# Decoder layer on one core: the first two phases rebuilt (weight splits, score blocks, token load, row copies)

## What is computed

```python
x = x + attn(layernorm(x))            # 16 heads of 8, causal softmax, then a layernorm of its own and Wo
x = x + xattn(ctx, layernorm(x))      # one head of 128 over the 64 context tokens, biases bv, bq, bo
x = x + ffn(layernorm(x))             # 8 experts 128 -> 512 -> 128 with relu, b1, b2;
                                      # gates: alpha-entmax (alpha 1.5) of xt @ Wr + br, by 25 bisections
```

## Time and profile before

| what | us |
|---|---|
| median of 3 runs (785.18 to 788.53) | 788.36 |
| profiled execution | 785.36 |
| its span | 783.6 |
| phases 0 and 1, to the first expert product | 163.4 |
| one round of the loop (246.8 to 326.0 is the most of one) | 79.2 |
| PE busy | 693.9 (89%) |

### The profile page before, as it was taken

One profiled execution on the slowest core, in us unless ns is written; L12 is line 12 of the kernel. 1 busy time (PEld: TensorE's weight loads), 2 busy tenths in 40 slices (PEclk: granted clock), 3 DMA queues, 4 the chain that ended last, 5 costly groups with the idle time before them and its releaser, 6 DMA issues.

```text
span 783.6 us, 14820 instructions
## 1 busy us (share of the span) xinstructions
PE 693.9 (89%) x4769; PEld 493.9 (63%) x4769; DVE 454.5 (58%) x953; ACT 419.3 (54%) x800; POOL 349.7 (45%) x571
## 2 busy tenths in 40 slices
PE   4797374679998999999999999999999999988996
PEld 3553243456776677667766776677767775666774
DVE  3246133643698368845875578647954795455542
ACT  3121362148556764576556655675568546755443
POOL 5000244035535654464536353735374517453363
PEclk9977595569999999999999999999999999999998
DMA  6200421003500270017100710062006300500040
GB/s 200 55 1 10 128 58 28 2 16 74 133 2 17 47 173 1 15 25 172 24 3 14 168 50 2 15 143 74 2 15 137 81 2 3 122 17 0 19 104 13
DMA packets 36169, 42.44 MB, mean 54 GB/s; under 512 B 3860, under 2 KB 19745, under 8 KB 36133
## 3 DMA queue, kind: packets, MB, share of 16 engines
q1 hardware_dynamic: 36132, 41.99, 22.2%
HBM read 9.46 MB, written 2.10 MB: 15 GB/s over the span
## 4 chain that ended last, share of the span: by engine, by line
PE 44%; issue 26%; POOL 12%; DVE 7%; ACT 6%; SPq 2%; DMA 1%; POOLq 1%; ACTq 0%; DVEq 0%
PE h_ps L849 6%; POOL y_sb L802 4%; PE h_ps L851 4%; PE h_ps L850 4%; POOL acc L805 3%; PE sbuf_s L931 3%; PE y_ps L849 3%; PE y_ps L851 3%; PE y_ps L850 3%; POOL rstd_a L734 3%; PE sbuf_s L917 3%; DVE negmax L1335 2%; ACT ln L1128 2%; ACT prob L1167 2%; PE sbuf_m L931 2%
## 5 line engine op out<-in xcount | busy, mean ns | idle before, releaser
L1419 DVE SCALAR_TENSOR_TENSOR h_lo<-h_ps,h_hi 128x512 fp32r<-128x512 f32 x256 | 173.9, 685 | 152.3 <-ACT h_hi L1186 150.4
L1186 ACT ACTIVATE h_hi<-h_ps 128x512 fp32r<-128x512 f32 x256 | 153.5, 600 | 159.8 <-PE h_ps L851 157.5
L725 POOL TENSOR_SCALAR_AFFINE_SELECT prob<-prob 128x512 f32<-128x512 f32 x128 | 81.0, 642 | 147.0 <-ACT prob L1167 141.6
L1335 DVE TENSOR_REDUCE negmax<-sbuf_s 128x4 f32<-128x1024 f32 (+1 forms) x96 | 114.3, 1218 | 18.1 <-PE sbuf_s L900 18.1
L1167 ACT ACTIVATE prob<-sbuf_s 128x768 f32<-128x768 f32 x128 | 99.4, 814 | 47.2 <-PE sbuf_s L917 47.1
L849 PE MATMUL h_ps<-fT_lo,w_hi 128*128 128x512 f32 x256 | 118.6, 463 | 5.0 <-DVE fT_lo L1311 2.7
L849 PE MATMUL y_ps<-h_lo,w_hi 128*128 128x512 f32 x256 | 103.1, 403 | 1.2 <-ACT y_sb L1193 1.2
L851 PE MATMUL h_ps<-fT_hi,w_hi 128*128 128x512 f32 x256 | 101.6, 397 | 0.0
L850 PE MATMUL h_ps<-fT_hi,w_lo 128*128 128x512 f32 x256 | 101.5, 397 | 0.0
L851 PE MATMUL y_ps<-h_hi,w_hi 128*128 128x512 f32 x256 | 101.1, 395 | 0.0
L850 PE MATMUL y_ps<-h_hi,w_lo 128*128 128x512 f32 x256 | 101.0, 395 | 0.0
(11 more groups left out here) (327 smaller groups left out, 1120.8 us busy)
## 6 DMA issues: line engine op xcount, KB each, us to landing
gate_b<-gT SPq DMA_DIRECT2D x64, 256.0 KB, 4.9
stacks<-qk SPq DMA_DIRECT2D x96, 128.0 KB, 2.6
x_t<-in_x_dram SPq DMA_DIRECT2D x8, 256.0 KB, 2.8
gate_b<-in_L_ffn_W_dram SPq DMA_DIRECT2D x1, 2048.0 KB
stacks<-qk SPq DMA_DIRECT2D x128, 4.0 KB
x_r<-in_x_dram SPq DMA_DIRECT2D x8, 256.0 KB, 4.0
out_dram<-sums SPq DMA_DIRECT2D x8, 256.0 KB, 4.1
prob<-in_ctx_dram SPq DMA_DIRECT2D x1, 512.0 KB, 4.1
```

The costliest lines, as they stand in the source:

```text
L725: pool.affine_select(out=v, in_=v, compare_op=ALU.is_ge, fill=0.0, base=0, pattern=[[0, 2], [0, 2], [1, P]], channel_multiplier=-1).then_i ...
L1186: act.activation(h_hi[:, c % HB, :], h_ps[:, c % 2, :], ACT.Relu).then_inc(hhi_made, 1)
L1335: dve.tensor_reduce(negmax[:, tile, heads].rearrange("p (g j) -> p j g", j=NJ)[:, j:j + 2, :], halves[buf].rearrange("p j (g s) -> p j g s ...
L1419: dve.scalar_tensor_tensor(out=h_lo[:, c % HB, :], in0=h_ps[:, c % 2, :], scalar=0.0, in1=h_hi[:, c % HB, :], op0=ALU.max, op1=ALU.subtrac ...
```

## The change

Phases 2 to 6 keep their tables. Phases 0 and 1 get new ones, and these things are different in them:

1. W1 is split first, straight from `stage`: four steps w1r, ACT rounds two experts to w1_hi, POOL subtracts to w1_lo. The centring of a w1 step then is two one-pass products on w1_hi and w1_lo, and b1 is a third over two rows (high part and rest). w1 0 and 1 stay in phase 0, w1 2 to 7 are in phase 1. W2's load waits for the splits alone (new step w2L). The last w2 split waits for w1 7 and vo 1.
2. A step "pairs" makes the two-row biases of b1 and xbo. Its source is a copy of b1 to all 128 rows; ACT rounds it, DVE forms the rest on odd rows. It stands behind T1 on ACT.
3. The next tokens' load (XL) is issued before the stack copies; SZ 1 and NZ 1 are in phase 0.
4. MAX and SC work in half blocks in phases 0 and 1: each step has two heads a group and its own buffer.
5. Half of phase 0's stack copies is issued by ACT (new step KS).
6. In every phase the rows of MT go in two copies of 16 rows in place of eight of 4; negmax is laid out for that.
7. ka 0 and 1, kp 1 and vo 1 move from phase 0 to phase 1, and vp 0, xwo and V move ahead in phase 0.

```diff
@@ tables (some rows)
-    Step("Q", 0, "s", pe=2, act=2, dve=2),
-    Step("K", 0, "t", pe=3, act=3, dve=3, sp=3),
-    Step("V", 0, "m", pe=3.1, dve=3.1),
+    Step("pairs", 0, "-", act=0.2, dve=6.2),
+    Step("XL", 1, "-", sp=1),
+    Step("Q", 0, "s", pe=1, act=2, dve=2.1),
+    Step("xwo", 0, "y", pe=3.1, act=1, dve=3),
+    Step("V", 0, "u", pe=3, dve=2),
+    Step("K", 0, "y", pe=6, act=5.1, dve=6.1, sp=4),
+    Step("KS", 0, "-", act=6.1),
...
@@ SP
+            sp.dma_start(whole[:, 0:2 * F], b1.rearrange("(a n) f -> a (n f)", n=2).unsqueeze(1)
+                         .to_broadcast([NE // 2, 32, 2 * F])).then_inc(b_loaded, 16)
...
-                for g in range(NG):
-                    for r, src in enumerate((nm_hi, nm_lo)):
-                        sp.dma_start(words(qs[3 + 4 * r:P:ROWS, g, t]), words(src[g * NJ:(g + 1) * NJ, t]))\
-                          .then_inc(nm_stacked[b], 16)
+                for r, src in enumerate((nm_hi, nm_lo)):
+                    sp.dma_start(words(qs[3 + 4 * r:P:ROWS, :, t]), words(src[:, t])).then_inc(nm_stacked[b], 16)
...
-                    for e in range(NE):
-                        drained(sp, ph, "w1", e)
+                if name == "w2L":
+                    sp.wait_ge(w1_lo_made, NE // 2)
...
@@ POOL
+                if name == "w1r":
+                    c = slice(2 * n, 2 * n + 2)
+                    pool.wait_ge(w1_hi_made, n + 1)
+                    pool.tensor_tensor(w1_lo[:, c, :], stage[:, c, :], w1_hi[:, c, :], ALU.subtract).then_inc(w1_lo_made, 1)
...
@@ PE
+            def heads_of(ph, n):
+                return range(NJ) if ph.f is not None else range(2 * (n % 2), 2 * (n % 2) + 2)
...
-                    last = centred(dst, stage[:, n, :], rows[at:at + 1, n % 2 * F:(n % 2 + 1) * F], at)
+                    r = slice(n // 2 * 32, n // 2 * 32 + 2)
+                    pe.matmul(dst, centre_r, w1_hi[:, n, :], start=True, stop=False)
+                    pe.matmul(dst, centre_r, w1_lo[:, n, :], start=False, stop=False)
+                    last = pe.matmul(dst, share_r[r, :], b1_pairs[r, n % 2 * F:(n % 2 + 1) * F], start=False, stop=True)
...
@@ ACT
+                if name == "pairs":
+                    act.wait_ge(b_loaded, 32)
+                    act.activation(b1_pairs, whole[:, 0:2 * F], ACT.Copy).then_inc(pairs_hi, 1)
+                    act.activation(xbo_pair, whole[:, 2 * F:2 * F + E], ACT.Copy).then_inc(pairs_hi, 1)
...
+                if name == "KS":
+                    drained(act, ph, "Q")
+                    drained(act, ph, "K")
+                    act.wait_ge(const_made, 7)
+                    for r, src in enumerate((qk[:, 0:4:2, :], qk[:, 1:3, :], qk[:, 0:4:3, :])):
+                        for g in range(1, NG, 2):
+                            act.dma_start(words(stacks[r:P:4, :, g, :]), words(src[g * 32:(g + 1) * 32, :, :]))\
+                               .then_inc(stacked, 16)
```

More of the change, by code:

```diff
@@ L291 @@
+    Step("MAX", 10, "s", pe=30.1, dve=31),
+    Step("NA", 2, "-", act=31),
+    Step("SC", 0, "s", pe=31.2, act=31.1, pool=31),
+    Step("MAX", 11, "t", pe=31.1, dve=31.1),
+    Step("MT", 1, "v", pe=33.1, dve=32, sp=34),
+    Step("T3", 0, "m", pe=33, act=33, dve=33),
+    Step("SC", 1, "t", pe=35, act=34, pool=34),
+    Step("SC", 2, "s", pe=35.1, act=34.1, pool=34.1),
+    Step("SC", 3, "t", pe=35.2, act=35, pool=35),
 ]
@@ L333, in in_order, with earlier @@
         return sorted([s for s in self.all if s[place] is not None], key=lambda s: s[place])
+    def earlier(self, engine):
+        return Phase(0, z=0).in_order(engine) if self.parts == self.KINDS[1] else []
     def fill(self, step):
+        if step[0:2] not in self.order[step.buf]:
+            return Phase(0, z=0).fill(step)
         return self.before[step.buf] + self.order[step.buf].index(step[0:2])
     def find(self, name, n=0):
-        return next(s for s in self.all if s[0:2] == (name, n))
+        return next(s for s in self.all + (FIRST_Z if name in TABLES else []) if s[0:2] == (name, n))
     def steps(self, engine, slot):
@@ L891, in max_scores @@
                 for at, g in enumerate(gs):
-                    for j in range(NJ):
+                    for j in js:
                         r = slice(ROWS * j, ROWS * (j + 1))
@@ L911, in scores @@
                     pair = ph.z if n < EARLY else ph.a
-                    pe.wait_ge(nm_stacked[b], pair * 128 + 128)
+                    pe.wait_ge(nm_stacked[b], pair * 32 + 32)
                 for first in (True, False):
-                    for j in range(NJ):
+                    for j in js:
                         r = slice(ROWS * j, ROWS * (j + 1))
@@ L918, in scores @@
                                          qs[r, g, b * S + q0:b * S + q0 + w], start=True, stop=True)
-                        if not first and j == 1:
+                        if not first and j == 1 and len(js) == NJ:
                             last.then_inc(full["s"], 1)
@@ L937, in step @@
                 name, n, buf = s[0:3]
-                if name in ("MAX", "SC") and n % 2:
+                quad = name in ("MAX", "SC") and ph.f is not None
+                if quad and n % 2:
                     return
@@ L1298, in step @@
                     level_xwq()
+                if name == "pairs":
+                    dve.wait_ge(ident_made, 2)
+                    mark(dve.tensor_reduce(odd[:, :], ident[:, 1:P:32], AX.X, ALU.add, negate=True))
+                    settle()
+                    dve.wait_ge(pairs_hi, 2)
+                    for v, w in ((b1_pairs, whole[:, 0:2 * F]), (xbo_pair, whole[:, 2 * F:2 * F + E])):
+                        ins = dve.scalar_tensor_tensor(out=v, in0=v, scalar=odd[:, 0:1], in1=w, op0=ALU.mult, op1=ALU.add)
+                    ins.then_inc(pairs_made, 1)
                 if name == "SZ":
-                    dve.wait_ge(x_loaded, ph.z * 16 + 16)
+                    dve.wait_ge(x_loaded, (ph.z + n) * 16 + 16)
                     statistics("z", x_t)
-                    if ph.a is None:
+                    if ph.a is None and n == 0:
                         setup()
```

307 lines of the change are left out of this document (168 added, 139 removed).

## The result

The changed kernel takes **756.29 us** (median of 4 executions, 753.84 to 758.48) against 786.77 for the kernel before beside it: a ratio of 0.962, 95% interval 0.957 to 0.967. Measured again later, it took 751.73 us (749.54 to 754.40), ratio 0.955 (0.952 to 0.958). The forecast was 753.0, range 742 to 765. The profiled execution took 753.84 us, its span 752.1, so 31.5 us less than the profiled one of before; the sum of the prediction had 33.4.

The account below looks back on a forecast made before the run. PE bounds the loop, so only the first 163.4 us could gain. Gains 7.0 + 16.2 + 11.7 - 5.8 + 4.3 = 33.4 take 785.36 to 752.0 (755.0 from the median); it said 753, range 742 to 765.

Parts of the forecast that it names:

- Part 1: Start to first score block: 39.4 us before, 32.4 forecast, with steps moved out of the way; gain 7.0.
- By that rule a quarter of the engines give 90 GB/s and 5.8 us: Part 1, copy of b1: if slow, "pairs" ends near 17, not 13.4; part 1 up to 1 us longer, sum 753.
- ACT idle before "pairs" beyond 16 us: Part 1: listed as a sign that the forecast is wrong, ACT waiting past 16 us before rounding b1.
- I take SP's price, since the copies are the same: Part 1: ACT's six stack copies cost 0.66 us of issue each, as on SP, and run beside SP's six.
- sixteen passes of 128 columns at V's 0.21 us are 3.4 us: Part 1, vo on PE: starts at 29.0, takes 3.4 us, so the first score block starts at 32.4.
- Part 2: Twelve score maxima to last score step: 26.8 us for 43.0, by one-pass W1, fewer W1 steps and half blocks; gain 16.2.
- Part 3: Handover to pair 1: 11.7 us before, 0 forecast, since the next tokens load before the stacks; gain 11.7.
- Part 4: Attention of pair 0: 27.5 us for 21.7, five steps moved in, ACT the bound at the high clock; loss 5.8.
- Part 5: After attention, to the first feed-forward product: 43.3 us for 47.6, half blocks removing stalls; gain 4.3.
- the low clock in part 4: Rival: the clock stays low in part 4, PE binds at 36 us, +9, 762; chance 0.17, together with a hidden stall.
- More is gained: Rival: PE runs at 2.4 GHz through parts 2 and 5 too, giving 744; chance 0.15 (738 to 747).
- the slow merged copy: Rival: the merged MT row copy makes PE wait 5 us in each of eight phases, giving 792; chance 0.02.

Follow-up runs that it names:

- the first kernel of "What is best": Changed kernel with b1 in four copies, vo's row product first as one product, eight stack copies on SP and four on ACT, first W1 split behind kp: 746.76 us.
- b1 in four copies alone: Changed kernel with the copy of b1 to 128 rows issued as four copies of 32 rows: 747.97 us, ratio 0.950.
- whole blocks: Changed kernel with whole score blocks for maxima and scores in phases 0 and 1, one low half of W1 behind a maximum on DVE: 767.16 us.
- late tokens: Changed kernel with load, statistics, deviation and normalising of the second pair's tokens put back to the start of phase 1: 768.29 us.
- rounding of b1 late: Changed kernel with ACT's rounding of the pairs of b1 moved behind K's high half, b1 still one slow copy: 751.20 us.
- stacks on SP: Changed kernel with all twelve stack copies of the first pair on SP, none on ACT: 752.76 us, ratio 0.956.
- warm: Changed kernel with products that nobody reads put in PE's idle time of phase 0: 756.76 us, ratio 0.961.
- eight rows: Changed kernel with the rows of MT issued as eight small copies per half pair again, in place of two: 758.66 us, ratio 0.963.
- best, W1 by float32: Fastest one-pass kernel (b1 in four copies, vo's row product first, eight and four stack copies) with W1 products by float32: 744.28 us, ratio 0.947.
- W1 by float32: Changed kernel with the two large products of each of the eight W1 steps by float32, row product still one pass: 758.79 us, ratio 0.964.
- the same, again: Changed kernel with the W1 products by float32, run and profiled a second time: 758.78 us.

## Why the prediction was right, and where it was not

**That everything lies before 163.4 us** held. The span behind the first feed-forward product is 620.2 us before, 621.1 after, and 620.9 to 622.9 in the other kernels. The loop's round did not change: between two loads of tokens lie 81.15 us before (250.06 to 331.21) and 81.13 after (215.36 to 296.49).

**Part 1** was mis-sized by 5.1 us, in three terms. The largest was "By that rule a quarter of the engines give 90 GB/s and 5.8 us, "pairs" ends near 17 in place of 13.4, part 1 is up to 1 us longer". The rule of the Trainium skill (DMA: Bandwidth & Descriptors, Rules for kernel authors) points the right way: the trace can't show on which engines the copy ran, but four copies with an outermost dimension of 32 landed 6.1 us sooner than one with 4. The size was wrong. The copy landed 11 us after its issue, not 5.8. A likely reason is that it did not have its engines to itself (behind it stood 2.5 MB of other loads, and the DMA share from 16 to 20 us is 1.06); no run takes those loads away. And a late "pairs" was priced as a shift of one step, but the whole chain of Q, K and stacks stands behind it on ACT: 4.5 us of the first score block. One of the prediction's own signs of being wrong, "ACT idle before "pairs" beyond 16 us", did come. Second, "I take SP's price, since the copies are the same" and six and six side by side: 0.88 and 0.90 us each instead of 0.66, some 1.4 us more, inside the range of 0 to 8 that the prediction carried for ACT. Third, "sixteen passes of 128 columns at V's 0.21 us are 3.4 us": vo took 4.9. A row product of two rows between products of 128 rows costs PE some 0.4 us more than its own columns. With one product of 512 columns ahead of the groups, in the first kernel of "What is best", they follow each other 0.64 us apart and vo takes 3.5 us (25.80 to 29.3). The three add up to more than 5.1, since other terms were too long: with b1 in four copies alone the first score block comes at 32.99, with all three terms changed at 29.47, 2.9 us before the forecast. Which these were I did not look for.

**Part 2** (26.8, measured 25.4 and 24.3 in the two profiles of the changed kernel) was right in its steps: reductions 1.22 to 1.25 us apart in the wide blocks, PE setting the pace in the narrow ones, MAX 11 behind w1 1. The undone edits price it: whole blocks +6.1 us, the rows of MT in eight copies +2.0. W1 by one pass was the term over-valued: the prediction said that one step "held PE for some 2.1 us and at the low clock for up to 4, and the eight for some 21", and put most of the gain of part 2 on this together with half blocks. By float32 part 2 takes 0.8 to 2.5 us more, and the whole kernel 2.5 to 7. Of the 17.6 us that part 2 lost, these three leave 7 to 9 over. I put them down to moving six of the eight steps out of it, into parts 4 and 5 (the forecast has 2.1 us of PE and more for each); no run undoes the moves, so that this share is argued and not shown.

**Part 3** was exact as a sum (11.7 to 0) and mixed as a cause: 8.4 are the early tokens, and the rest is by difference the merged rows, which the prediction gave no term of their own: "8 issues become 2 per half pair, at 0.5 us each", and nothing in the loop. The price of an issue (1.09 us for two) and the nothing in the loop are as it said.

**Part 4** was too long by 3.8. The failed step is that ACT, with 19 us of work, "is the bound at the high clock". ACT had 18.60 us of work, as forecast, but in the windows PE is busy for 23.05 of 23.74 us at 0.90 of full, and for 21.01 of 21.81 in the kernel with four b1 copies, at 1.00: PE is the bound. The prediction had the number that mattered, PE's 21 us of work at the high level, and the stretch at full clock lasts 21.8. The walk gave ACT's chain 27.5 us, 3.8 more than the part took; which of its waits were too long was not looked up. The rise of the clock, forecast at 66 us, came at 67.7 in the first profile and 63.6 in the second.

**Part 5** (43.3, measured 44.3 and 46.1) followed its clock. Over the executions of kernels with one-pass W1, 0.51 gave 47.2 and 47.3, 0.53 and 0.54 gave 46.1 and 46.6, 0.57 gave 45.7, 0.59 gave 44.3 twice, 0.62 and 0.63 gave 43.3 and 43.4 (part 2 of the late tokens is without PE's wait of 8.4):

| kernel | first score block | part 2 | part 4 (clock) | part 5 (clock) |
|---|---|---|---|---|
| changed | 37.5 | 25.4 | 23.7 (0.90) | 44.3 (0.59) |
| changed, again | 37.6 | 24.3 | 22.5 (0.96) | 46.1 (0.53) |
| b1 in four | 33.0 | 25.1 | 21.8 (1.00) | 43.3 (0.62) |
| rounding of b1 late | 35.0 | 27.5 | 23.2 (1.00) | 43.4 (0.63) |
| stacks on SP | 34.7 | 27.5 | 23.7 (1.00) | 44.3 (0.59) |
| warm | 36.5 | 27.5 | 23.6 (0.90) | 47.3 (0.51) |
| eight rows | 37.6 | 27.4 | 28.6 (0.71) | 47.2 (0.51) |
| late tokens | 37.0 | 27.6 | 28.4 (0.72) | 47.3 (0.51) |
| whole blocks | 37.6 | 31.5 | 29.5 (0.79) | 46.6 (0.54) |
| best, one-pass W1 | 29.5 | 24.1 | 22.4 (0.96) | 45.7 (0.57) |
| W1 by float32 | 37.1 | 26.2 | 24.4 (1.00) | 39.9 (0.83) |
| the same, again | 37.2 | 26.8 | 25.6 (0.93) | 44.4 (0.75) |
| best, W1 by float32 | 29.3 | 26.7 | 24.4 (1.00) | 50.3 (0.64) |

So part 5 moved by 4 us with its clock, and part 4 by 5 where the clock was 0.71 or 0.72, about as the range said ("-4 to +9"). In part 4 the granted clock does not order the times by itself: 23.2 and 23.7 us stand beside 1.00, in executions in which PE came in at its slow pace (its first 16 value products take 1.51 us, as at the low level), and 21.8 stands beside 1.00 where it came in fast (0.86). **The rivals:** the low clock in part 4 did come in two kernels (0.71 and 0.72) and cost 5 us, not 9; the 744 of "More is gained" was nearly reached by the kernel with b1 mended (747.97) and reached by the two of "What is best" (746.76 and 744.28), though by part 1 and not by the clock; the slow merged copy is out by its own experiment.

What stays open: what in a kernel's work decides when the clock falls. Each fall that was looked up came while PE ran at its fast pace, but PE had done so for very different times: in the changed kernel from 53.9 to the fall at 57.5, from 67.7 to that at 88.2 and from 118.9 to that at 125.7, with the late tokens from 26.6 to 27.6, with the unread products from 19.0 at the latest to 34.4. In the two profiles of the changed kernel with float32 products there was no fall in part 2. The runs do not show why.

## What to carry to other kernels

When two engines take turns over one pair of buffers, half the work in each buffer is worth more than a faster instruction: undoing that one condition cost over 10 us. Where a small constant is broadcast from DRAM, look at the outermost dimension of the copy and at who stands behind its consumer in the queue; one line gave 4 to 8 us of time, and one number in the order 2.5 us of part 1. And before reading a gain of 3 us out of one profile, compare the stretches' granted clock and profile the same kernel twice.
